# Attention scores: both accumulation steps on one row tile, side jobs between a block's rounds, tokens added by transposes

## What is computed

```python
tokens = x.reshape(B, C, N).transpose(0, 2, 1)            # 8, 1024, 128
qkv = (tokens @ w_proj + b_proj).reshape(B, N, 8, 48)      # 8 heads of 16
q, k, v = jnp.split(qkv, 3, axis=-1)
attn = softmax(einsum('bihd,bjhd->bijh', q, k) * 16 ** -0.5, axis=2)
res = einsum('bijh,bjhd->bihd', attn, v).reshape(B, N, 128)
x = res @ w_out + b_out + tokens
t = t + spiking_attention(layernorm(t))
t = t + expert_mlp(layernorm(t))
```

## Time and profile before

| | us |
|---|---|
| median of 3 runs | 1154.07 |
| lowest, highest run | 1153.24, 1156.74 |
| the profiled execution's own time | 1151.01 |
| its span, first to last instruction | 1148.7 |
| TensorE busy in the span | 1081.2 (94%) |
| VectorE, ScalarE, GpSimd busy | 874.8, 780.5, 323.0 |

### The profile page before, as it was taken

The page is one execution under the profiler, slowest core; times in us unless marked ns, Lnnn a source line. Parts: engine busy times, 40 slices in busy tenths (PEclk is TensorE's granted clock), DMA queues, the critical chain, the costliest instruction groups (busy, mean ns, idle before and its releaser), DMA issues. The chain is left out here.

```text
span 1148.7 us, 23592 instructions
## 1 busy us (share of the span) xinstructions
PE 1081.2 (94%) x8048; PEld 528.4 (46%) x8048; DVE 874.8 (76%) x1975; ACT 780.5 (68%) x1693; POOL 323.0 (28%) x381
## 2 busy tenths in 40 slices
PE   5999999999999999999999999999988997899994
PEld 2223333333333333333333333333367666899993
DVE  4979978988987988898798789886057886664445
ACT  2158777777777777777777778778756753655553
POOL 4041031113104102310510311004432665675550
PEclk7599999999999999999999999999999996999997
DMA  5609206502800730470182064000060112223317
GB/s 127 126 10 191 46 2 133 113 8 73 151 23 2 175 70 1 102 144 1 34 173 39 1 133 94 2 1 20 1 169 24 38 34 70 62 77 87 82 41 297
DMA packets 66315, 85.52 MB, mean 74 GB/s; under 512 B 15656, under 2 KB 49064, under 8 KB 64664
## 3 DMA queue, kind: packets, MB, share of 16 engines
q1 hardware_dynamic: 60856, 72.91, 29.1%
q0 software_dynamic: 4320, 8.89, 2.3%
q10 hardware_dynamic: 1024, 2.23, 0.6%
HBM read 57.08 MB, written 26.65 MB: 73 GB/s over the span
## 5 line engine op out<-in xcount | busy, mean ns | idle before, releaser
L733 DVE TENSOR_REDUCE neg_half<-slot 128x1 f32<-128x512 f32 x1024 | 633.9, 682 | 104.0 <-PE slot L508 85.7
L647 ACT ACTIVATE probs<-ring 128x512 f32<-128x512 f32 x1024 | 528.7, 603 | 137.3 <-PE ring L517 135.0
L517 PE MATMUL ring<-stack_q,stack_k 50*128 50x512 bf16 (+1 forms) x2048 | 421.0, 383 | 1.9
L559 PE MATMUL acc<-probs,v_sb 128*32 128x512 f32 x2048 | 274.1, 607 | 0.0
L517 PEld LDWEIGHTS ring<-stack_q,stack_k 50*128 50x128 bf16 (+1 forms) x2048 | 152.4, 93 | 258.4 <-issue 110.7
L510 PE MATMUL slot<-twin_k,twin_q 48*128 48x512 bf16 x512 | 183.2, 393 | 20.1 <-DMA twin_q<-parts_dram 12.0
L508 PE MATMUL slot<-stack_k,stack_q 48*128 48x512 bf16 x512 | 163.0, 394 | 2.8 <-DVE neg_half L733 2.8
L1661 ACT ACTIVATE mask<-bank,w_of 128x128 f32<-128x128 f32 x284 | 80.8, 368 | 57.6 <-PE bank L1627 57.6
L423 POOL CAST m_parts<-neg_max 128x16 bf16<-128x16 f32 x32 | 6.3, 196 | 383.7 <-DVE neg_max L739 383.7
L510 PEld LDWEIGHTS slot<-twin_k,twin_q 48*128 48x128 bf16 x512 | 47.6, 93 | 94.6 <-DVE neg_half L733 72.6
L1600 POOL DMA_INDIRECT rows_tok<-mask,x_in x71 | 68.3, 961 | 56.7 <-DVE mask L1695 51.6
(11 more groups left out here) (170 smaller groups left out, 1098.2 us busy)
## 6 DMA issues: line engine op xcount, KB each, us to landing
parts_dram<-parts SPq DMA_DIRECT2D x30, 384.0 KB, 5.7
stack_k<-parts_dram SPq DMA_DIRECT2D x16, 384.0 KB, 5.9
stack_q<-parts_dram SPq DMA_DIRECT2D x32, 192.0 KB, 7.0
x_in<-rows_in SPq DMA_DIRECT2D x71, 64.5 KB, 2.3
xp<-in_x SPq DMA_DIRECT2D x8, 512.0 KB, 5.2
stack_k<-parts_dram SPq DMA_DIRECT2D x16, 256.0 KB, 3.7
xr<-in_x SPq DMA_DIRECT2D x8, 512.0 KB, 3.8
out<-zt SPq DMA_DIRECT2D x16, 256.0 KB, 2.2
```

What stands on the lines that cost most here:

```text
L517: return pe.matmul(out[:, :], stack_k[s % STACK_BUFS][rows, h, kt * P:(kt + 1) * P], stack_q[s % STACK_BUFS][rows, half, h, :], start=star ...
L559: mm = pe.matmul(acc[32 * h:32 * h + 32, :], v_sb[s // G % 2][:, kt, s % G * HG + h, :], probs[:, j % PROBS, h, :], start=(kt == 0), stop= ...
L647: act.activation(probs[:, j % PROBS, h, :], ring[n % S_BANKS][:, :], ACT.Exp).then_inc(s_empty[n % S_BANKS], 1)
L733: dve.tensor_reduce(neg_half[q % 2][:, half, k:k + 1], slot[n % M_BANKS][:, :], AX.X, ALU.max, negate=True).then_inc(m_empty[n % M_BANKS], 1)
```

## The change

Heads are dealt to the row tiles: even heads of a group lie at partitions 0 to 49, odd heads at 64 to 113. Each row tile holds both runs A and BB of its heads in one buffer, side by side along the free dimension, so both steps of a score run on one row tile, one after the other, and TensorE's wait for its own first step goes. A maximum is taken on the row tile of its head, for both halves of the keys; twin_q, twin_k and their loads go. A stack is loaded by 14 DMAs instead of 9, with the same bytes; a set of row maxima goes out in 4 DMAs instead of 2. A block is cut into a front and a rear of three rounds each, and all side jobs but `mturn` move from 10t+4 to 10t+10.5, which is between front and rear of the next block. A solo now takes two maxima. The last change is L628, where the token tile is added by a matmul in transpose mode.

```diff
 PARTS = 3
-RUN_A = (0, 0, 3)
-RUNS_B = [(0, 1, 2), (0, 2, 1)]
-A, BB = 0, 64
+A, BB = 0, 1
+RUNS_A = [(A, 0, 0, 0, 3)]
+RUNS_B = [(BB, 0, 0, 1, 2), (BB, 2 * DH, 0, 2, 1)]
+TILE_ROW = (0, 64)
+HT = HG // 2
-STACK_BUFS, TWIN_BUFS = 3, 2
-STACK_DMAS, TWIN_DMAS = 9, 6
+STACK_BUFS = 3
+STACK_DMAS = 14
...
-ROUNDS = ((0, 4), (1, 5), (2, 0), (3, 1), (4, 2), (5, 3))
+FRONT = (("score", 0, A), ("max", 1, 0)), (("score", 0, BB), ("score", 1, A)), (("max", 0, 0), ("score", 1, BB))
+REAR = (("score", 2, A), ("max", 1, 1)), (("score", 2, BB), ("score", 3, A)), (("max", 0, 1), ("score", 3, BB))
...
+def place_of(m):
+    q, k = m // QB, m % QB
+    tile, k = k % 2, k // 2
+    return q, tile, k // (KT // 2), k % (KT // 2)
...
-        put(10 * t, "block", (t // BLOCKS, t % BLOCKS, m, maxima))
+        put(10 * t, "front", (t // BLOCKS, t % BLOCKS, m, maxima))
+        put(10 * t + 1, "rear", (t // BLOCKS, t % BLOCKS, m, maxima))
         put(10 * t + 12, "pv", (t // BLOCKS, t % BLOCKS))
         m += maxima
         if t % 2 and m < 2 * t + 2 + AHEAD_MAX and maxima:
-            for n in range(2):
-                put(10 * t + 7, "solo", (m + n,))
+            put(10 * t + 7, "solo", (m,))
             m += 2
     for s in range(STEPS):
         for at, kind, args in side_jobs(s):
             t = s * BLOCKS + at
-            put(10 * t + 4, kind, args)
+            put(10 * t + 4 if kind == "mturn" else 10 * t + 10.5, kind, args)
...
-    first += [("solo", (n,)) for n in range(QB + 1)] + [("mturn", (0,))]
-    first += [("solo", (n,)) for n in range(QB + 1, AHEAD_FIRST)]
+    first += [("solo", (n,)) for n in range(0, QB + 2, 2)] + [("mturn", (0,))]
+    first += [("solo", (n,)) for n in range(QB + 2, AHEAD_FIRST, 2)]
...
     if kind == "solo":
-        return [(("max", (args[0], tile)), tile, 1) for tile in range(2)]
+        return [(("max", (args[0] + tile, half)), tile, 1) for half in range(2) for tile in range(2)]
...
-    stack_q = [sb(f"stack_q{i}", [P, 2, HG, HALF], BF16) for i in range(STACK_BUFS)]
-    stack_k = [sb(f"stack_k{i}", [P, HG, N], BF16) for i in range(STACK_BUFS)]
-    twin_q = [sb(f"twin_q{i}", [RUN_ROWS, 2, HG, HALF], BF16) for i in range(TWIN_BUFS)]
-    twin_k = [sb(f"twin_k{i}", [RUN_ROWS, HG, HALF], BF16) for i in range(TWIN_BUFS)]
+    stack_q = [sb(f"stack_q{i}", [P, 2, HT * N], BF16) for i in range(STACK_BUFS)]
+    stack_k = [sb(f"stack_k{i}", [P, 2, HT, N], BF16) for i in range(STACK_BUFS)]
...
+    def load_q(eng, dst, b, g, runs, done, cols=slice(0, N)):
+        for tile, base in enumerate(TILE_ROW):
+            for run, row, cq, _, n in runs:
+                rows = slice(base + row, base + row + n * DH)
+                src = parts_dram[b % 2, 0, g, cq:cq + n].rearrange("c (d h) n -> (c d) h n", d=DH)[:, tile::2, :]
+                if run == BB:
+                    eng.dma_start(dst[rows, run, :].rearrange("p (h n) -> p h n", h=HT)[:, :, cols],
+                                  src[:, :, cols]).then_inc(done, 16)
+                    continue
+                for half in range(2):
+                    eng.dma_start(dst[rows, run, half * HT * HALF:(half + 1) * HT * HALF]
+                                  .rearrange("p (h n) -> p h n", h=HT),
+                                  src[:, :, half * HALF:(half + 1) * HALF]).then_inc(done, 16)
...
-                for r in range(MROWS):
-                    sp.dma_start(stack_q[u % STACK_BUFS][RUN_ROWS + r:RUN_ROWS + r + 1, half, :, :]
...
+                for tile, base in enumerate(TILE_ROW):
+                    for r in range(MROWS):
+                        row = base + RUN_ROWS + r
+                        first = r * QB + tile * (QB // 2)
+                        sp.dma_start(stack_q[u % STACK_BUFS][row:row + 1, A, half * HT * HALF:(half + 1) * HT * HALF]
...
-            load_k(sp, twin_k[0], 0, 0, RUNS_TWIN, s_lead, HALF)
...
-            load_twin(1)
...
-                    load_twin(2 * b + 2)
...
-                    load_twin(2 * b + 3)
...
             def ones_rows(i):
-                pool.memset(stack_k[i][32:64, :, :], 1.0).then_inc(s_ones, 1)
+                for base in TILE_ROW:
+                    pool.memset(stack_k[i][base + 32:base + 64, A, :, :], 1.0).then_inc(s_ones, 1)
...
                     elif not last:
-                        score(free_bank(use), *args, (A, BB)[tile], True).then_inc(s_begun[tile], 1)
-                        begun[tile] += 1
-                        first[use] = s_begun[tile], begun[tile]
+                        score(free_bank(use), *args, A)
                     else:
-                        pe.wait_ge(*first[use])
-                        out = ring[S_USE[use] % S_BANKS]
-                        score(out, *args, (A, BB)[tile], False).then_inc(s_fill[tile], 1)
+                        score(ring[S_USE[use] % S_BANKS], *args, BB).then_inc(s_fill[tile], 1)
...
                         pe.matmul(dst, o_n[:, k // 2, tok % HALF:tok % HALF + P], w_o[:, :], start=True, stop=False)
-                        mm = pe.matmul(dst, xr[:, tok:tok + P], ident[:, :], start=False, stop=True)
+                        mm = pe.matmul(dst, xr[:, tok:tok + P], ident[:, :], start=False, stop=True,
+                                       is_transpose=True)
```

More of the change, by code:

```diff
@@ L126, in halves @@
     if kind == "solo":
-        return [(("max", (args[0], tile)), tile, 1) for tile in range(2)]
-    if kind != "block":
+        return [(("max", (args[0] + tile, half)), tile, 1) for half in range(2) for tile in range(2)]
+    if kind not in ("front", "rear"):
         return []
     s, j, m, maxima = args
[L131 to L137, removed]
+    out = []
+    for pair in FRONT if kind == "front" else REAR:
+        for what, n, step in pair:
+            if what == "score":
+                out.append((("score", (s, 4 * j + n)), n % 2, int(step == BB)))
+            elif maxima:
+                out.append((("max", (m + n, step)), n, 1))
     return out
@@ L513, in score @@
-            def score(out, s, i, base, start):
+                q, tile, ht, qt = place_of(m)
+                u = q // 2
+                rows = slice(TILE_ROW[tile], TILE_ROW[tile] + RUN_ROWS)
+                return pe.matmul(out[:, :], queries(u, BB, q % 2, ht)[rows, qt * P:(qt + 1) * P],
+                                 stack_k[u % STACK_BUFS][rows, BB, ht, half * HALF:(half + 1) * HALF],
+                                 start=True, stop=True)
+            def score(out, s, i, run):
                 j, h = i // HG, i % HG
@@ L515, in score @@
                 half, kt = j // KT, j % KT
-                rows = slice(base, base + RUN_ROWS + (MROWS if base == A else 0))
-                return pe.matmul(out[:, :], stack_k[s % STACK_BUFS][rows, h, kt * P:(kt + 1) * P],
-                                 stack_q[s % STACK_BUFS][rows, half, h, :], start=start, stop=not start)
-            begun = [0, 0]
-            first = {}
+                tile, ht = h % 2, h // 2
+                rows = slice(TILE_ROW[tile], TILE_ROW[tile] + RUN_ROWS + (MROWS if run == A else 0))
@@ L524, in rounds @@
+                return pe.matmul(out[:, :], stack_k[s % STACK_BUFS][rows, run, ht, kt * P:(kt + 1) * P],
+                                 queries(s, run, half, ht)[rows, :], start=run == A, stop=run == BB)
             def rounds(job):
-                if job[0] == "block":
+                if job[0] == "front":
                     s, j = job[1][:2]
@@ L569, in _ @@
                     continue
-                if kind in ("block", "solo"):
+                if kind in ("front", "rear", "solo"):
                     rounds(job)
@@ L658, in _ @@
                 kind, args = job
-                if kind == "block":
+                if kind in ("front", "rear"):
                     for use in filled_by(job):
```

95 lines of the change are left out of this document (38 added, 57 removed).

## The result

The changed kernel took 1123.18 us (median of 4 runs, 1123.10 to 1125.39), the kernel before 1153.65 beside it (1152.49 to 1156.74): a ratio of 0.9736, 95% interval 0.9714 to 0.9759, or 30.5 us less. The forecast was 17 us less (1137, range 1123 to 1155): the right sign, with the result at the range's lower edge.

The account below looks back on a forecast made before the run. TensorE bounds the attention stage (busy 49.67 of 50 us). +9.7 (switch) - 10.7 (ring waits) - 3.3 (output blocks) - 3 (L610's blocks) - 7.5 (transposes) - 2.3 (start) = -17, from 1154 to 1137 us; range 1123 to 1155.

Parts of the forecast that it names:

- plain blocks that gain 10 us: Rival: blocks without a job lose their stall and go to 2.41 us, some 10 us more, 1127 us; chance 0.10.
- The block times put down as signs: Signs if right: plain 2.52 us, projection 3.58, V 3.6, output 3.35, L610's 3.1 to 3.4.
- The extra switch: Jobs between third and fourth round add one change of array shape: 0.11 us each, +9.7 us for 88 jobs.
- the dear switch: Rival: third round to job costs more than 0.11 us; no gain from 0.25, 1164 us at 0.34; chance 0.14.
- The ring: TensorE's 54 score waits for ScalarE to empty a side job's bank (17.4 us) go through the jobs' placement: -10.7 us.
- The stall under a job in the midst: In 30 output-job blocks the 0.11 us stall goes, as maxima slots are free by then: -3.3 us.
- L610's blocks: 31 blocks with four transposes: period 3.4 or 3.1 against 3.45 us, about -0.1 on average, extra switch included: -3 us.
- Transposes: Output job's token matmuls become transposes: 0.125 us saved each, two per job, 30 jobs: -7.5 us.
- the rival that they give nothing: Rival: transposes and start give nothing, 1147 us, or 1160 if each matmul-transpose change costs 0.11; chance 0.12.
- Plain blocks: Blocks without a job: the chain from first to sixth round stands, the period stays at 2.52 us: 0.
- The start: First maximum waits until 23.68 for eight loads, which shrink from 960 to 576 KB: -2.3 us, near 21.4.
- The rows of maxima: Rival: their loads come late and TensorE waits at a step's start, up to 8 x 1.5 us, 1149 us; chance 0.09.

Follow-up runs that it names:

- e2: The kernel before with its six rounds cut after the third and all side jobs but mturn put there, nothing else changed: 1141.95 us, ratio 0.9923.
- e1: The changed kernel with all side jobs back between two blocks: 1130.71 us, ratio to the kernel before 0.9812.
- e4: The changed kernel with side jobs back between blocks and tokens added by a plain matmul, leaving the layout alone: 1135.5 us, ratio 0.9874.
- f3: The changed kernel with the maxima four further ahead (AHEAD_MAX 30 instead of 26): 1124.4 us, ratio 0.9761.
- g2: The changed kernel with VectorE's minimum L744 issued behind the two maxima of the next front, from the fifth set on: 1121.01 us, ratio 0.9731.
- f2: The changed kernel with only oturn (transposes of the weighted sums) in the midst of the rounds, other jobs back between blocks: 1126.01 us, ratio 0.9761.
- g1: The changed kernel with oturn alone put back between blocks; projections, V, back and output jobs stay in the midst: 1124.41 us, ratio 0.9768.
- e3: The changed kernel with the tokens added by a plain matmul with the identity instead of transpose mode: 1132.36 us, ratio 0.983.
- f4: The changed kernel with maxima four further ahead and, in blocks without maxima, scores of two heads paired on the row tiles: 1123.69 us, ratio 0.9747.
- g3: The changed kernel with VectorE's minimum L744 issued behind all four maxima of the next block: 1121.6 us, ratio 0.9738.

## Why the prediction was right, and too small

**The sum in the steady blocks**: forecast -17 + 2.3 = -14.7, measured 696.65 - 715.38 = -18.7. That the total lies in the range is luck in part. The forecast's own range was 1129 to 1145; 1123 was put in for plain blocks that gain 10 us, and these gained some 2. What filled the place is the gain of the early and last blocks (2.7 and 3.7), which no rival named, some 2 more in the blocks with jobs, and a profiled execution of before that lay 2.6 under its median. The same kernel once more (f1) has a median of 1119.47, under the range.

The block times put down as signs came out: projections 3.57, V 3.60, output 3.37, L610's 3.23 to 3.41 but for three of 29 (up to 3.78). They don't tell which part of the change made them.

*The extra switch*, forecast 0.11: 0.09 in every kernel with a job in the midst, 0.10 in e2. Right, and the dear switch falls (it needed 0.25). The rule weighed there, from the Trainium skill, TensorEngine Tiling (Array Packing), Key Properties, that a change of mode drains the engine, is borne out no further than in the trace of before: the third round lasts 0.37 and the job starts 0.31 after the round did.

*The ring: "The 54 waits go"*, -10.7 (17.4 - 54 x 0.12 is 10.9; nothing hangs on the 0.2). They went, but the step names the wrong part of the change. The layout alone removes them (e1 and e4, one left in each); the placement alone does so for long jobs, and makes the short ones worse (e2). The error is in the sentence on the layout: "The same 12 matmuls of 512 columns in six rounds [...]: 0". The order within the rounds had changed as well: the fourth score's first step goes from the fourth round to the fifth, and the prediction followed that order for the maxima only, not for the banks.

*The stall under a job in the midst*, -3.3 for the 30 output blocks. The 0.08 is real, but it is won in projection, V and back blocks as well, whose fifth-to-sixth stall is there as soon as the ring's is gone (e1: 0.30). So each of the jobs other than oturn pays 0.01 to 0.02 net for its new place. Three terms of the sum (+9.7, -10.7, -3.3) have the wrong owners and a total 2 us short: -4.3, where the blocks show 6.1 to 6.5 less without the transposes. With the transposes the terms came to -11.8; the four kinds of blocks show 24 x 0.16 + 14 x 0.07 + 14 x 0.09 + 28 x 0.24 = 12.8 less (differences before rounding).

*L610's blocks*, -3: 29 x 0.14 = 4.1 less. The step said "the first two maxima now go ahead of the job on VectorE. What remains is L739", and f3 and g2 bear that out, for 0.10 of the 0.23 left over (3.33 to f3's 3.10). Missing is the neighbour: the placement wins 6.4 (e1), 2.3 of which repays what the layout takes, and most of it needs the jobs of the blocks ahead in the midst too (f2, g1).

*Transposes*, -7.5: 6.3 (e4 to e1) and 6.7 (e3 to changed). Right; the rival that they give nothing, or cost four switches a job, falls.

*Plain blocks*, "stays at 2.52: 0": 2.50, and 2.53 instead of 2.56 with a turn of the maxima. The chain is the one described, the reduction starts 0.02 earlier, which was not followed further; some 2 us. Of the rival that they gain to 2.41 a fifth is there.

*The start*, -2.3. The first maximum, 2.7 earlier in this execution:

```profile
20.98 1.03 PE L519 MATMUL slot<-stack_k,stack_q 48*128 48x512 bf16 x3 [10.12 <-DMA stack_q<-parts_dram]
```

Over the eleven traces with the new loads it stands at 20.48 to 22.69, mean 21.36, over the two with the old ones at 23.68 and 22.96: -2.0, and "near 21.4" was said. Right.

*The rows of maxima*, rival with up to 1.5 us in each of eight images: once, in the first. SP's queue and TensorE, where the first score of the second step waits for the four DMAs, the normal distance from PV being 1.00:

```profile
96.26 2.77 SPq L361 DMA_DIRECT2D stack_q<-m_rows  x4
...
97.84 1.07 PE L562 MATMUL acc<-probs,v_sb 128*32 128x512 f32 x8
100.17 0.37 PE L528 MATMUL ring<-stack_q,stack_k 50*128 50x512 bf16 x1 [1.27 <-issue]
```

2.33 - 1.00 = 1.3 us. Every other kernel with the new loads and the same number of maxima ahead has it, at 1.0 to 1.7 us; neither kernel with the old loads has it. In later images the 14 loads and 4 rows end well ahead of their score, as reckoned from the earlier trace rows:

```profile
465.36 3.77 SPq L326 DMA_DIRECT2D stack_k<-parts_dram  x6
...
475.21 2.77 SPq L361 DMA_DIRECT2D stack_q<-m_rows  x4
...
479.83 0.39 PE L528 MATMUL ring<-stack_q,stack_k 50*128 50x512 bf16 x1
```

The score at 479.83 follows its PV by 1.00 with the rows issued by 477.98.

**Outside the steady blocks** the forecast had the start alone. The last 14 blocks give 3.7 (layout, e4; the old pairs leave one tile idle in four of six rounds once no maxima are left), the early four 2.7. Neither stretch is in the prediction's sum: its rows are of the start and of the middle. Sum by the trace: -3.6 to the first PV, -2.7, -18.7, -3.7, and +1.5 in the rest: -27.2. The profiled execution of before lay 2.6 under the median it is compared with, that of the changed kernel at its median; so the medians differ by 30.5.

## What to carry to other kernels

When a change reorders matmuls, follow each shared buffer through the new order by itself, banks and slots alike: a bank asked for one round later can be worth as much as a move of whole jobs (6 us against 5 in the steady blocks here), and two parts that remove the same wait don't add there, even where their totals happen to. A total that agrees with a theory is not yet that theory's: e1's total agreed with the wrong one, and the blocks told. Read the edges, first and last blocks, as well as the middle; what a steady block hides, a block without its side work shows. And a job between two consumers' fills costs a switch but gives the consumer time; count that for the next block too.

## What was not expected of the hardware

The early blocks are 2.7 us shorter, some 2.0 of it through the clock: by the starts in the two traces the first PV, where the clock has not yet risen (0.61 from 55 to 60 us), takes 1.48 instead of 1.00, the round ahead of the fourth block 0.53 instead of 0.31, and the fourth block 3.79 instead of 2.50. The other 0.7 is in the blocks with the first projections. Stretches of the kernel before (columns as in the earlier trace rows; the last three are the granted clock, the DMA share and GB/s):

```profile
68.00:72.00 4.00, 2.94 (x16) 0.72 (x16) 3.04 (x7) 1.00 (x2) 3.08 (x6) 1.00 0.00 0
72.00:77.00 5.00, 4.84 (x29) 1.39 (x32) 3.66 (x7) 2.70 (x6) 4.28 (x5) 0.66 0.00 0
```

the same place of the changed kernel:

```profile
64.00:68.00 4.00, 3.33 (x16) 0.84 (x15) 3.92 (x8) 1.72 (x3) 3.63 (x6) 1.00 0.00 0
68.00:73.00 5.00, 5.00 (x39) 1.43 (x37) 4.48 (x8) 4.07 (x10) 3.75 (x5) 1.00 0.02 3
```

and of e1:

```profile
66.00:70.00 4.00, 3.16 (x17) 0.75 (x13) 2.97 (x6) 1.44 (x3) 2.75 (x6) 1.00 0.00 0
70.00:74.00 4.00, 4.00 (x22) 0.77 (x21) 2.95 (x6) 1.97 (x4) 3.78 (x5) 0.67 0.00 0
```

In the kernel before, TensorE was busy 2.94 of 4 us beside solos that wait for VectorE, and then ran a part of the next 5 us at the lower level (1.2 GHz; rounds at 0.40 to 0.43). In the changed kernel it was busy 3.33 of 4 and the clock stayed at 1.00. The busy share does not settle it: cut from 62 to 66 us, the changed kernel is busy 3.15 of 4 and stays at 1.00 in the next 4 us too, and e1, after 3.16 of 4, falls to 0.67. The lower level shows at this place in before, e4 and e2 once and in e1 and f2 twice, and in none of the eight profiles on the new layout with the projections in the midst of the rounds (changed, its repeat, e3, f3, f4, g1, g2, g3). That the jobs' place decides it is shown by e1 and g1; what in it the chip reacts to was not tried. The other surprise is the mixture of transposes and matmuls in one accumulation: 0.10 from a transpose to the next matmul and 0.23 from that matmul to the next transpose (428.17, 428.27, 428.50 above), where a matmul behind a matmul takes 0.22 (e3): no cost for the change shows.
